# A gated scan with a mixture of experts beside it: VectorE's per-half sums, products and norms placed one block of 16 steps later

## The reference, cut to what matters

```
dt = soft_clamp(softplus(xn @ Wdt.T + bdt), 0.001, 0.1, 0.5)
B, C = xn @ WB.T, xn @ WC.T
dA = exp(soft_clamp(dt[..., None] * A, -8, 8, 0.5)); dB = dt[..., None] * B[:, :, None, :]
h0 = 0                                            # (4, 256, 16)
def step(h, inp):
    h = dA_t * h + dB_t * x_t[..., None]
    h = h * min(20 / (sqrt(sum(h * h)) + 1e-8), 1)
    return h, einsum('bdn,bn->bd', h, C_t) + Dp * x_t
```

## Time and profile before

| | us |
|---|---|
| median of 3 runs | 1767.44 (1767.29 to 1767.97) |
| the profiled execution | 1766.3 |
| its span, first to last instruction | 1764.2 |
| VectorE busy in the span | 1550.5 (88%) |
| TensorE busy | 1302.9 (74%) |
| ScalarE busy | 1227.6 (70%) |
| GpSimd busy | 770.1 (44%) |

### The profile page before, as it was taken

The page is one execution under the profiler, slowest core; times in us unless marked ns, Lnnn a source line. Parts: engine busy times, 40 slices in busy tenths (PEclk is TensorE's granted clock), DMA queues, the critical chain, the costliest instruction groups (busy, mean ns, idle before and its releaser), DMA issues.

```text
span 1764.2 us, 33864 instructions
## 1 busy us (share of the span) xinstructions
PE 1302.9 (74%) x9352; PEld 1143.0 (65%) x9352; DVE 1550.5 (88%) x9455; ACT 1227.6 (70%) x3152; POOL 770.1 (44%) x1254
## 2 busy tenths in 40 slices
PE   5674434389879797987979797987979697835661
PEld 5553433378768686876868686876868586734551
DVE  6588888888979998997989899998989799997778
ACT  4587547388687887868687877878787777746451
POOL 3146666533434343433434343343434344468842
PEclk8577767699999898988989899998999899967885
DMA  9921111200111020111102002011101110012245
GB/s 335 340 92 49 46 43 42 96 25 24 41 55 37 25 71 24 37 59 31 31 17 91 18 26 71 27 41 34 55 24 49 40 31 19 19 34 73 75 126 195
DMA packets 95533, 113.29 MB, mean 64 GB/s; under 512 B 8432, under 2 KB 85360, under 8 KB 95344
## 3 DMA queue, kind: packets, MB, share of 16 engines
q1 hardware_dynamic: 87696, 94.13, 16.6%
q0 software_dynamic: 6144, 16.79, 3.0%
q10 hardware_dynamic: 1504, 0.22, 0.1%
HBM read 60.91 MB, written 50.20 MB: 63 GB/s over the span
## 4 chain that ended last, share of the span: by engine, by line
DVE 47%; PE 23%; ACT 9%; issue 8%; POOL 8%; DMA 3%; POOLq 0%; SPq 0%; DVEq 0%; ACTq 0%
DVE arena L756 10%; DVE arena L733 8%; DVE arena L745 7%; DVE arena L741 7%; DVE arena L727 7%; DVE arena L760 4%; PE ps L1213 4%; PE ps L1197 4%; POOL arena L536 4%; ACT arena L875 4%; PE ps L1185 4%; POOL xg L515 3%; PE ps L1160 3%; PE ps L1179 2%; DVE arena L730 2%
## 5 line engine op out<-in xcount | busy, mean ns | idle before, releaser
L536 POOL TENSOR_TENSOR arena<-arena,neghalf 128x1 f32<-128x1 f32 x1025 | 591.7, 577 | 881.1 <-DVE arena L730 812.0
L756 DVE SCALAR_TENSOR_TENSOR arena<-arena 128x128 f32<-128x128 f32 x1024 | 362.6, 354 | 53.3 <-POOL arena L536 53.1
L1185 PE MATMUL ps<-arena,pick 128*128 128x128 f32 x2048 | 306.7, 298 | 39.5 <-ACT arena L971 20.1
L1185 PEld LDWEIGHTS ps<-arena,pick 128*128 128x128 f32 x2048 | 285.1, 214 | 51.3 <-ACT arena L971 38.2
L971 ACT ACTIVATE arena<-ps,arena 128x128 f32<-128x128 f32 x1024 | 292.2, 377 | 35.1 <-PE ps L1185 34.7
L1179 PE MATMUL ps<-ident,arena 128*128 128x128 f32 x1024 | 211.8, 335 | 136.9 <-ACT arena L875 132.0
L1197 PE MATMUL ps<-arena,wf 128*128 128x256 f32 x1280 | 302.8, 387 | 8.1 <-issue 8.1
L741 DVE CUSTOM_DVE_ANT_0 arena<-arena 128x128 f32<-128x128 f32 x1024 | 294.2, 287 | 10.1 <-PE ps L1144 7.7
L1213 PE MATMUL ps<-wp,arena 128*128 128x256 f32 x1280 | 296.2, 385 | 5.4 <-ACT arena L979 5.1
L733 DVE CUSTOM_DVE_ANT_0 arena<-arena 128x128 f32<-128x128 f32 x1024 | 299.1, 292 | 0.0
L727 DVE TENSOR_TENSOR arena<-arena 128x128 f32<-128x128 f32 x1024 | 289.9, 283 | 4.5 <-POOLq L531 4.5
(11 more groups left out here) (147 smaller groups left out, 1380.3 us busy)
## 6 DMA issues: line engine op xcount, KB each, us to landing
xg<-zeros SPq DMA_DIRECT2D x10, 1024.0 KB, 9.1
xrow<-xg SPq DMA_DIRECT2D x40, 256.0 KB, 2.8
yg<-arena SPq DMA_DIRECT2D x40, 256.0 KB, 2.2
arena<-in_x SPq DMA_DIRECT2D x16, 512.0 KB, 9.3
wf<-in_c_fc SPq DMA_DIRECT2D x8, 1024.0 KB, 5.0
wp<-in_c_proj SPq DMA_DIRECT2D x8, 1024.0 KB, 5.9
arena<-dx SPq DMA_DIRECT2D x66, 64.0 KB, 2.3
ys<-arena SPq DMA_DIRECT2D x66, 64.0 KB
```

The costliest lines, as they stand in the source:

```text
L536: g.tensor_tensor(sv[:, slot, 1:2], mx, neghalf[:, 0:1], ALU.pow).then_inc(s_ready, 1)
L756: v.scalar_tensor_tensor(hr[:, slot, :], vv, sv[:, before, 1:2], ur[:, slot, :], ALU.mult, ALU.add)\
L1185: last = t.matmul(ps[2][:, j * P:(j + 1) * P], pick[:, q * QUAD + j, :], xin, start=True, stop=True)
```

## The change

The three ranges of the planner move up by one block each, for all halves from 2 on. Nothing else is edited.

```diff
         for h in range(2, HALVES):
-            for table, pieces, lo_, hi_ in ((sum_at, 1, 4 * h - 9, 4 * h - 7), (input_at, 2, 4 * h - 6, 4 * h - 4), (norm_at, 1, 4 * h - 3, 4 * h - 1)):
+            for table, pieces, lo_, hi_ in ((sum_at, 1, 4 * h - 8, 4 * h - 6), (input_at, 2, 4 * h - 5, 4 * h - 3), (norm_at, 1, 4 * h - 2, 4 * h)):
```

## The result

| | before | changed |
|---|---|---|
| median, us | 1767.37 | 1715.99 |
| runs | 4, 1763.6 to 1768.0 | 4, 1712.6 to 1717.1 |
| profiled execution | 1766.3 | 1716.85 |
| its span | 1764.2 | 1714.7 |

The ratio is 0.971, 95% interval 0.969 to 0.973: 51 us faster, where 56 were forecast (1711, range 1696 to 1736).

A forecast was written before the change was run, and what follows sets the result against it. TensorE, nearly as full as VectorE, was taken to set the stretch's end: 33.3 us of holds and 12 of low clock plus 11.3 in reserve give 56.6 off 1766.3, so 1709.7, median 1711, range 1696 to 1736.

The forecast's parts named there:

- All 75.2 us before L623 and L629: VectorE's idle time before the sum (70.1 us) and the product (5.1), all claimed to go with the move.
- The orders argued from the queues: In ScalarE's queue, logs and soft clamp precede quads the scan needs, so moved pieces and their readers get no new wait.
- 18.6 us at L741: Part of VectorE's 75.2 us said to return as scan waits for ScalarE's quad 0 or TensorE's output of the next block.
- 1463.3: Time in us when TensorE's output 56 was to come, from 1508.6 before; it rules the scan, 56.6 us earlier than 1519.9.
- TensorE's holds by the scan: TensorE's waits caused by VectorE, blocks 12 to 56: 28.2 us before L1140 and 5.1 before L1213, claimed to go, minus 33.3.
- The low clock after holds: TensorE's slower products behind six holds in the stretch, claimed to speed up by 12 us in sum, bounds 4 and 14.
- Block 12, taken as fixed at 399.65: Start of TensorE's block 12, claimed to stay, since no wait for VectorE stands before it after the experts began.
- the 1.95: Us saved behind each of six TensorE holds, from 16 products of L1213 taking 5.57 against 3.62 a moment later.
- The granted clock of the stretch: TensorE's granted clock from block 12 to block 56, claimed to rise from 0.94.
- A: Rival: VectorE is the bound and all 75.2 us come back, giving 1692 us; chance 0.10.
- B: Rival: TensorE comes no earlier, its holds become waits for ScalarE, and the scan gains only 11.3 us, 1756; chance 0.10.
- C: Rival: TensorE under unbroken load gets a lower clock and the kernel is slower, 1810 us at 0.85; chance 0.03.

The follow-up runs named there:

- the other five runs of full weight: Kernels with sums, products or norms moved differently and all work kept: sum only 0.971, norm stays 0.971, sum by 4 steps 0.979, products to .03 0.980, products only 1.008.
- the light version: The changed kernel without the second half of each expert's down product on TensorE (4 of 8 chunks): 1688.1 us, ratio 0.959.

## Why the prediction was right

**What goes.** All 75.2 us before L623 and L629 went, and no new wait appeared before sums, products or norms, nor before ScalarE's readers of them. The orders argued from the queues (the logs stand ahead of quad 0, and so on) held in every half.

**What comes back, and where.** Forecast 18.6 us at L741, at the last steps of blocks 15, 19, ... or the first step behind; measured 26.6, of which 22.9 there or at 11.15, 1.2 at 12.00 and 2.1 at 44.07. Blocks 31 and 55 have none. That the scan goes on as output 56 ends held to 0.1 us; that it ends at 1463.3 was 8 us too early.

**The terms.** TensorE's holds by the scan were put at 33.3; its time that is neither busy nor held by L875 fell from 59.6 to 30.8, by 28.8. Of the 28.2 before L1140, 1.9 remained, and of the 5.1 before L1213, 2.3: ScalarE was behind there on its own account. This is the mis-sized term. The low clock after holds was put at 12; TensorE's busy time fell by 11.5. Block 12, taken as fixed at 399.65, began at 402.7. Of these 3.0 us, 1.2 were there when the first expert rows landed (342.9 and 344.1), and the rest is low clock: from there to block 12 TensorE was busy 47.4 us instead of 45.2 with the same work. Whether the change has a part in it is not shown; block 12 began at 399.1 to 401.5 in the other five runs of full weight in the table. So -4.5, -0.5 and -3.0 make 48.6 of 56.6, against the measured 48.4 at the scan's step 56.00. The sum gave 1709.7 for the profiled execution and it took 1716.85, 7 us more; that the median is only 5 above the forecast is luck, since it lies 0.9 below the profiled execution here and lay 1.1 above it before.

**The term that came out partly by luck.** Not all of the 11.5 stands where the 12 were put. The five long holds at L1140 gave what was said: comparing instruction by instruction, the products in the 12 us behind each cost 1.4 to 2.9 us less, 10.4 in all. But the hold before L1213, from whose row the 1.95 was read, gave 0.2. It shrank from 5.1 to 2.3 us, the clock behind it was still low, and the same 16 products took 5.41 instead of 5.57:

```profile
760.65 5.41 PE L1213 MATMUL ps<-wp,arena 128*128 128x256 f32 x16 [2.31 <-ACT arena L979]
760.70:766.00 5.30, 5.30 (x17) 4.38 (x18) 5.16 (x35) 0.87 (x2) 2.25 (x4) 0.68 0.36 148
```

In its place a shorter hold, of 2.0 us in block 26, which the prediction did not count, gave 1.8.

**The sign that was too small to see.** The granted clock of the stretch was to rise from 0.94, and the rows show 0.94 again. With one more digit the traces have 0.936 before and 0.945 in the changed kernel: it rose, but by less than the rows can tell.

**The rivals.** A (all of it, 1692) needed TensorE lighter, as the light version shows: its ratio of 0.959 is 1695 us on the first chip. B (only the reserve, 1756) fell with the 28.8. C did not occur. One wrong turn was to count the product's wait of 5.1 as part of what the change gives. In the run with the sums alone it is still there, 5.8 us at 10.03, and the time is the same. The error is in rival A and in the 18.6, not in the 1711, which TensorE's queue sets.

## What to carry to other kernels

A wait in front of an early, unhurried piece of a saturated in-order queue holds everything behind it; ask for the result later, and look first at what its producer has queued ahead of it. Before counting such a wait as gain, follow the next-fullest engine from one fixed event to another: its holds that the first engine caused, with the low clock behind them, plus the reserve between the two is what can be gained. And once two engines take turns as the pace, more waits that are not the latest of their round are free, as the run with the sums alone shows; that an instruction moved from ahead of such a wait to behind it is not, is only my reading of one run.

## What was not expected of the hardware

Short pauses of TensorE cost more than their length. In the kernel before, eight holds of 2.04 to 5.13 us before L1140 and L1213 were each followed by 4 us at a mean granted clock of 0.50 to 0.70. In the changed kernel six of them are down to 0.5 us or nothing, one is shorter and one stays, and the same instructions took 11.5 us less. In the version with the decays cut by time steps TensorE got its decays 5.4 us earlier in each half, but with a second pause behind, and was busy 947.6 us in place of 930.0. At block 28 its first 16 up products took 5.27 us, where the changed kernel, starting 5.5 later, took 4.65. That the second pauses cost this is my reading; no run tells them apart from the first.
